# One ScalarE unit reordered: first weighing, then decays, then the evacuation of the last tile's third turn

## The reference, cut to what matters

```
# layer 0, deformable 3x3 convolution
x = x + deform_conv(group_norm(x))        # 9 taps per pixel; each tap is a weighted sum of 4
                                          # corner pixels at learned places, then one matmul
# layer 1, a state-space block with 4 scan directions
dts = softplus(dt_w @ dtr + dt_b)
for l in range(4096):                     # per direction, 256 channels, 16 states
    h = exp(dts_l * A) * h + (dts_l * x_l) * B_l
    y = sum over states of h * C_l
x = x + block(group_norm(x))              # and two norms, a gate, two 3x3 convolutions
```

## Time and profile before

| | us |
|---|---|
| median of three runs | 15748.07 |
| lowest, highest | 15738.32, 15755.31 |
| profiled execution, its own time | 15757.44 |
| its span, first to last instruction | 15755.4 |

### The profile page before, as it was taken

How to read it: one execution, slowest core, us unless ns; L and a number is a source line. 1 busy time by engine, 2 the same in 40 slices (tenths; PEclk the granted TensorE clock), 3 DMA queues, 4 the chain that set the end, 5 groups by cost and what they waited for, 6 DMA issues and landing times.

```text
span 15755.4 us, 180094 instructions
## 1 busy us (share of the span) xinstructions
PE 12249.3 (78%) x47232; PEld 7550.1 (48%) x47232; DVE 11117.5 (71%) x12583; ACT 9633.9 (61%) x20979; POOL 5707.3 (36%) x4760
## 2 busy tenths in 40 slices
PE   5777878788787878878778787887878778787745
PEld 4454554545545354453545545454453545536312
DVE  3486785858758586784858858587684867858586
ACT  1275674756657476674756747576574756747533
POOL 6452341514425153350524415144250523516100
PEclk8878778787787878879788787877879788797867
DMA  5442342423334232342423324233342423424100
GB/s 162 117 132 76 115 118 74 130 86 105 105 88 130 75 117 84 108 126 65 131 79 113 112 80 131 88 103 98 97 129 67 124 82 111 124 67 131 62 1 13
DMA packets 669382, 1559.15 MB, mean 99 GB/s; under 512 B 77720, under 2 KB 350300, under 8 KB 659516
## 3 DMA queue, kind: packets, MB, share of 16 engines
q0 software_dynamic: 368640, 1208.25, 26.1%
q1 hardware_dynamic: 289980, 298.08, 6.4%
q10 hardware_dynamic: 9216, 33.56, 0.5%
HBM read 1333.44 MB, written 206.14 MB: 98 GB/s over the span
## 4 chain that ended last, share of the span: by engine, by line
PE 40%; DVE 24%; DVEq 15%; issue 10%; ACT 7%; POOL 2%; ACTq 1%; DMA 1%; SPq 0%; POOLq 0%
PE psum L1144 6%; DVEq L906 6%; PE psum L1078 5%; DVE arena L910 4%; PE psum L1276 4%; PE psum L1088 4%; PE psum L1267 3%; DVEq L898 3%; PE psum L1097 2%; DVE arena L915 2%; DVE arena L881 2%; DVE arena L877 2%; DVE arena L879 2%; DVE arena L932 2%; PE psum L1048 2%
## 5 line engine op out<-in xcount | busy, mean ns | idle before, releaser
L645 POOL DMA_INDIRECT gathered<-cell_table,index x2880 | 3245.8, 1127 | 2990.3 <-PE psum L1078 1978.3
L645 POOL DMA_INDIRECT arena<-cell_table,index x1440 | 1969.0, 1367 | 2057.5 <-PE psum L1078 1760.9
L428 ACT COPY samples_t<-psum 128x384 f32<-128x384 f32 x1536 | 716.9, 467 | 2203.2 <-PE psum L1078 1957.8
L1088 PE MATMUL psum<-samples_t,pack 128*128 128x128 f32 x9216 | 1850.5, 384 | 273.3 <-ACT samples_t L428 273.3
L1177 PE MATMUL psum<-arena,pack 32*128 32x512 f32 x1024 | 834.9, 907 | 1468.8 <-DVEq L929 1468.8
L1088 PEld LDWEIGHTS psum<-samples_t,pack 128*128 128x128 f32 x9216 | 1725.1, 289 | 464.7 <-ACT samples_t L428 464.7
L1078 PE MATMUL psum<-pack,gathered 128*128 128x128 f32 x11520 | 1572.6, 295 | 439.5 <-DVE gathered L819 297.7
L1078 PEld LDWEIGHTS psum<-pack,arena 128*128 128x128 f32 x6912 | 1324.8, 216 | 1063.6 <-issue 1063.3
L1078 PE MATMUL psum<-pack,arena 128*128 128x128 f32 x6912 | 1537.1, 408 | 370.8 <-DVE arena L1004 243.7
L441 ACT ACTIVATE arena<-arena,weight 128x128 f32<-128x128 f32 x5760 | 1734.6, 390 | 7.4 <-DMA arena<-cell_table,index 7.4
L441 ACT ACTIVATE gathered<-gathered,weight 128x128 f32<-128x128 f32 x5760 | 1730.0, 389 | 0.7 <-DMA gathered<-cell_table,index 0.7
(11 more groups left out here) (164 smaller groups left out, 19704.5 us busy)
## 6 DMA issues: line engine op xcount, KB each, us to landing
cell_table<-arena SPq DMA_DIRECT2D x64, 2112.5 KB
gathered<-cell_table,index POOLq DMA_INDIRECT x2880, 3.8
arena<-in_x SPq DMA_DIRECT2D x16, 2048.0 KB, 7.7
image<-in_x SPq DMA_DIRECT2D x16, 2048.0 KB, 7.7
x_dram<-image SPq DMA_DIRECT2D x16, 2048.0 KB, 10.2
arena<-x_dram SPq DMA_DIRECT2D x16, 2048.0 KB, 7.9
out<-arena ACTq DMA_DIRECT2D x64, 512.0 KB, 3.9
arena<-cell_table,index POOLq DMA_INDIRECT x1440
```

The lines of the kernel that those rows point to most:

```text
L645: pool.indirect_dma_start(gathered[m][:, n * CORNERS * C:(n + 1) * CORNERS * C], None, table, bass.IndirectOffsetOnAxis(ap=index[:, at:at ...
L1088: last = pe.matmul(psum[:, V_BANK, 0:TILE], wt("wconv")[:, n * C:(n + 1) * C], samples_t[:, n, :], start=n == 0, stop=n == TAPS - 1)
```

## The change

In ScalarE's `unit_of` the weighing of group 1 of tile t becomes the first work of a unit. The two decays follow. The evacuation of group 2 of tile t-1, which stood first, comes third. The softplus and the rest stay where they were. No instruction is added or removed, and no other engine's order changes. In the last image, where `with_next` is false, nothing changes.

```diff
                     t = k * PARTS + c
-                    if with_next and not is_(t, 0):
-                        evacuate(b + 1, t - 1, 1 - par, 2)
+                    if with_next:
+                        weigh(b + 1, t, 1)
 
                     def decays(step, n, j):
...
                     for j in range(2):
                         decays(0, slice(0, 1), j)
-                    if with_next:
-                        weigh(b + 1, t, 1)
+                    if with_next and not is_(t, 0):
+                        evacuate(b + 1, t - 1, 1 - par, 2)
                     if after:
                         soft(b, *after, 1 - par)
```

## The result

| | us |
|---|---|
| before, median of 4 runs | 15751.69 |
| changed kernel, median of 4 runs | 18077.61 (18070.61 to 18089.37) |
| ratio | 1.148, 95% interval 1.1466 to 1.1494 |
| predicted | 18,210 (17,150 to 18,950) |
| span of the profiled execution | 18078.6, before 15755.4 |

What follows compares the result with a forecast made beforehand. DVE was taken as the bound before, a loop through gathers, weighing and convolution after; 6.0 (even k) and 4.5 us (odd) more per unit, 164 per image over 15 images, gave 18,210 us, range 17,150 to 18,950.

Steps and rivals of the forecast that it cites:

- cover of 0.46 us: Before the change the convolution is ready 0.46 us before DVE asks for it at `add_tile`; all the cover for a delayed evacuation.
- The loop: Next gathers wait behind the convolution, and it behind weighing gathered data: 23.7 us per even unit, 23.6 odd.
- end of convolution to sixth gather: On PE and POOL, a turn and six gather issues up to the sixth's start: 10.2 us even k, 9.1 odd.
- landing, to the start of the weighing: Group 1's last gather, from issue to data landed before ScalarE weighs: 3.8 us, between 3.4 and 5.2.
- second loop: From `add_tile` through DVE's step sizes, decays, evacuation and convolution: 19.3 us for even k, 20.9 for odd.
- first delay: In unit 1 of each image, weighing from 2059.9 replaces an evacuation 3.2 us into the unit: about 6 us.
- Costs at nothing: Waits for step sizes, third turn, flag and softplus, and unit 0 of each image, were put at no added time.
- shorter-loop rival: Group 1 lands earlier, so the decays' wait for DVE's step sizes binds: 16,550 us, chance 0.11.
- The clock: PE stands still some 7 us before each convolution, so all were taken as long, 4.21 us rather than 2.31.
- lower end of 17,330: If every convolution on PE ran as the short one of 2.31 us, the time would be 880 us lower.
- rival of 15,590: Weighing fills ScalarE's idle time before the evacuation, and DVE's waits of 162 us go: faster, chance 0.04.
- The signs in the profile: Expected waits: ScalarE before L441 6 to 8 us, DVE before L826 4 to 6; L877 23 to 24 us apart.

Runs made afterwards that it cites:

- e9: Changed kernel without group 1's gathers for tiles 1 to 31, ordered weighing, evacuation, decays; 15,758.95 us, 1.0005 of the kernel before.
- e4: Changed kernel, order kept, without group 1's gathers for tiles 1 to 31, the same buffer weighed each unit; 16,278.79 us, 1.0333 of the kernel before.
- e5: Changed kernel with POOL gathering group 1 ahead of groups 0 and 2; 16,789.97 us, 1.0662 of the kernel before.
- e6: Changed kernel with one of group 1's twelve weighing instructions left, the wait on the gathers kept; 16,628.36 us, 1.0559 of the kernel before.
- e3: Kernel before, with ScalarE's unit reordered to weighing of group 1, evacuation, decays; 17,320.75 us, 1.0994 of the kernel before.
- e7: Changed kernel plus 14 matmuls into unused PSUM columns on PE between third turn and convolution; 17,572.04 us, 1.1154 of the kernel before.
- e2: Kernel before, with ScalarE's unit reordered to decays, weighing of group 1, evacuation; 18,088.8 us, 1.1484 of the kernel before.
- e1: Kernel before, with the decays moved ahead of the evacuation and group 1's weighing left behind both; 16,283.93 us, 1.0339 of the kernel before.
- e8: Kernel before, with four weighings of group 0 (its last tap) moved from DVE to the head of ScalarE's unit; 15,537.7 us, 0.9861.

## Why the prediction was right

**The bound.** The cover of 0.46 us behind the convolution was the right number to look for. ScalarE's idle time was no gain by this order: in the change what was put there had not landed, and in e9, where it was there, the time is 15,759, that of the kernel before, since DVE sets the pace.

**The loop.** The prediction named six terms. Beside them stand the turn shown for even k, and the means of 210 turns of even k and 225 of odd k in the trace:

| term | predicted, even | turn shown | mean, even | predicted, odd | mean, odd |
|---|---|---|---|---|---|
| end of convolution to sixth gather | 10.2 | 9.90 | 9.94 | 9.1 | 9.32 |
| landing, to the start of the weighing | 3.8 | 3.88 | 3.86 | 3.8 | 4.03 |
| weighing, to the decays | 3.60 | 3.53 | 3.52 | 3.60 | 3.52 |
| decays, to the evacuation | 1.33 | 1.22 | 1.22 | 2.37 | 2.21 |
| evacuation to convolution | 0.53 | 0.50 | 0.51 | 0.53 | 0.51 |
| convolution | 4.21 | 4.21 | 4.10 | 4.21 | 4.18 |
| sum | 23.7 | 23.24 | 23.15 | 23.6 | 23.78 |

The runs touched five of the six: e4 took the gathers and their landing out together, e5 brought the last gather forward, e6 shortened the weighing, e3 took the decays out, e7 shortened the convolution. Each gave back about its time, or as much as the second loop allowed. So the circle is shown and not only argued. No run touched the step from evacuation to convolution, or the landing apart from the issue. e5 and e6 came out near their forecasts (16,790 for 16,700 and 16,628 for 16,650).

**The sum.** Per image 164 us were predicted; 2,323 / 15 = 155 came. By the means of the whole trace even k was put at 6.0 us more per unit and is 5.4, odd k at 4.5 and is 4.7, and the first delay, put at 6 us, is about 4. So the excess of 9 us lies in the even units (15 x 0.6) and the first delay (2), and the odd ones take 2 back. In the even units each term but the landing is a little shorter than reckoned, most of all the first, 9.94 for 10.2. The units of k=0 in the image shown, (2061.1 - 1881.8) / 8 = 22.4 us on the mean, fit in: unit 0 among them pays nothing, as predicted. The step as a whole holds; its size was 6% too large. That the odd units miss the other way, and bring the total 2 us per image nearer, is luck.

**Costs at nothing.** They held. The step sizes were reckoned ready at 13.2 us against 17.6. ScalarE waited for them in 47 of 512 units, and these are the 32 of the last image and unit 0 of the 15 others; in none of the 465 units of the loop did it wait for them. DVE waited 26.8 us for the flag (32.4 before) and 24.4 for the softplus (24.5 before). But e2 shows how near that second loop is: with the weighing in it, it is as slow as the first. The shorter-loop rival was put at 16,550. It is real and e1 and e4 are its kernels, at 16,280. The difference is the convolution, which takes 3.64 us on the mean in e4 and had been put at 4.21: 0.57 x 465 = 265 us.

**The clock.** Taking the long convolution for all units was right within 0.08 us (mean 4.13, stage clock 0.67). The reason given for it, PE standing still before it, is only part: in the kernel before, where PE stood 0.57 us, 344 of 480 were long already, and the mean was 3.66. The lower end of 17,330 assumed the short one; e7 came part of the way with 17,572. The rival of 15,590, faster by filling idle time, had only the landing held against it. The landing did stop it here, but e9 shows that without it there is no gain either.

**The signs in the profile.** ScalarE's wait at L441 was said to be 6 to 8 us and is 7.4; DVE's at L826 4 to 6 and is 4.8 (2,437.7 / 505); units 23 to 24 us for both parities, and they are 23.0 and 23.9; first gather 2.5 to 3 us behind the convolution, where the mean is 2.5.

## What to carry to other kernels

Before work goes to the head of an in-order queue, find when its data land, counted from what releases their transfer. If that transfer is released by something behind the moved work, a wait becomes a loop, and the loop's full length, with each length of work in it, is the new period. Filling an engine's idle time pays only if the data are there and the work comes off the engine that sets the pace. The same slot cost 15% with a weighing whose data had not landed (the change), gave nothing with one whose data were there (e9), and gave 1.4% with one whose data were there and which had been DVE's (e8).

## What had not been expected

The prediction had the clock only as a doubt about the size. Fourteen matmuls whose results nobody reads made the changed kernel 506 us faster, with the granted clock of the stage up from 0.67 to 0.81 and a shorter convolution in the loop. And two orders with different bounds, the change (gathers' landing) and e2 (step sizes), ended 11 us apart. From the totals alone they would have passed for one cause; only the waits, 3,446.8 us at L441 in the one and 3,838.9 at L526 in the other, told them apart.
